# The mean square of a gated block: ones standing in four column groups, and a row turned back into a column

## The reference, cut to what matters

```
y = jnp.moveaxis(ys, 0, 1).reshape(b, l, D_INNER)          # D_INNER = 256
yn = y * jax.lax.rsqrt(jnp.mean(y * y, axis=-1, keepdims=True) + EPS) * norm_w
y = yn * jax.nn.silu(z)
return y @ Wout.T
```

## Time and profile before

| | |
|---|---|
| median of three runs | 737.92 us |
| the profiled execution's own time | 741.33 us |
| its span (first to last instruction) | 739.5 us |
| mean granted clock of TensorE | 0.967 |
| PE busy (TensorE, matmuls) | 661.4 us, 89% |
| PEld busy (TensorE, weight loads) | 542.4 us, 73% |
| DVE busy (VectorE) | 565.0 us, 76% |
| ACT busy (ScalarE) | 474.7 us, 64% |
| POOL busy (GpSimd) | 454.2 us, 61% |

### The profile page before, as it was taken

The page is one execution under the profiler, slowest core; times in us unless marked ns, Lnnn a source line. Parts: engine busy times, 40 slices in busy tenths (PEclk is TensorE's granted clock), DMA queues, the critical chain, the costliest instruction groups (busy, mean ns, idle before and its releaser), DMA issues.

```text
span 739.5 us, 19955 instructions
## 1 busy us (share of the span) xinstructions
PE 661.4 (89%) x5075; PEld 542.4 (73%) x5075; DVE 565.0 (76%) x1874; ACT 474.7 (64%) x1176; POOL 454.2 (61%) x648
## 2 busy tenths in 40 slices
PE   7978999999999999999998889999999999989800
PEld 5846766676666766676666579999999999988800
DVE  3388899989999999999999667667666667776644
ACT  3746767776687767676776437756655665666625
POOL 5023277777777777677776656767765555666643
PEclk9999999999999999999999799999999999999955
DMA  9180001110111011101110132333432224546243
GB/s 253 34 285 15 5 30 30 40 45 19 36 35 44 20 41 32 43 23 37 33 41 19 29 72 63 92 85 96 99 82 67 78 70 119 150 143 178 78 158 129
DMA packets 56399, 54.54 MB, mean 74 GB/s; under 512 B 9546, under 2 KB 45518, under 8 KB 56032
## 3 DMA queue, kind: packets, MB, share of 16 engines
q1 hardware_dynamic: 44704, 32.10, 16.4%
q0 software_dynamic: 8416, 16.93, 6.8%
q10 hardware_dynamic: 3168, 4.22, 1.6%
HBM read 31.05 MB, written 22.63 MB: 73 GB/s over the span
## 4 chain that ended last, share of the span: by engine, by line
PE 71%; DVE 11%; issue 9%; POOL 3%; DVEq 2%; ACT 2%; DMA 2%; SPq 0%; POOLq 0%; ACTq 0%
PE p L607 12%; PE pl L598 8%; PE pj L460 6%; PE p L598 4%; PE p L689 4%; PE p L659 4%; PE p L653 4%; PE p L697 3%; PE p L635 3%; PE pj L468 2%; PE p L668 2%; PE p L571 2%; PE p L557 2%; PE p L468 2%; PE pl L504 2%
## 5 line engine op out<-in xcount | busy, mean ns | idle before, releaser
L1634 POOL DMA_INDIRECT moe_rows<-xT x135 | 134.2, 994 | 91.2 <-DVE xT L1250 59.0
L1567 POOL DMA_INDIRECT sorted_rows<-pair,slot x128 | 128.7, 1006 | 32.5 <-issue 31.3
L1008 DVE SCALAR_TENSOR_TENSOR acc<-pj,conv_w_sb,acc 128x511 f32<-128x511 f32 (+2 forms) x192 | 142.4, 742 | 4.1 <-ACT acc L792 1.1
L607 PE MATMUL p<-w,xT 128*128 x1080 | 143.9, 276 | 1.8 <-DVE xT L1246 1.7
L927 ACT ACTIVATE xT<-pl,b_sb 128x128 f32<-128x128 f32 x360 | 103.1, 370 | 50.0 <-PE pl L598 48.4
L607 PEld LDWEIGHTS p<-w,xT 128*128 128x128 f32 x1080 | 132.0, 193 | 2.3 <-issue 2.2
L598 PE MATMUL pl<-xT 128*128 128x128 f32 x720 | 96.8, 278 | 2.4 <-DVE xT L1238 2.4
L598 PEld LDWEIGHTS pl<-xT 128*128 128x128 f32 x720 | 88.5, 194 | 3.1 <-issue 2.5
L1246 DVE TENSOR_TENSOR xT<-p,b_sb 128x128 f32<-128x128 f32 x135 | 39.1, 290 | 61.8 <-PE p L607 53.9
L792 ACT ACTIVATE acc<-pj,conv_b_sb,conv_w_sb 128x512 f32<-128x512 f32 x64 | 49.5, 773 | 33.5 <-PE pj L460 33.4
L927 ACT ACTIVATE xT<-p,b_sb 128x128 f32<-128x128 f32 x180 | 51.5, 370 | 25.1 <-PE p L598 24.1
(11 more groups left out here) (217 smaller groups left out, 1420.9 us busy)
## 6 DMA issues: line engine op xcount, KB each, us to landing
xT<-sorted_rows SPq DMA_DIRECT2D x135, 65.0 KB, 1.9
xres<-in_x SPq DMA_DIRECT2D x16, 256.0 KB, 3.1
w<-in_w SPq DMA_DIRECT2D x2, 2048.0 KB, 10.0
acc<-moe_rows SPq DMA_DIRECT2D x16, 256.0 KB, 4.0
xc<-moe_rows SPq DMA_DIRECT2D x16, 256.0 KB
out<-sz ACTq DMA_DIRECT2D x16, 256.0 KB, 2.4
moe_rows<-xT POOLq DMA_INDIRECT x135, 2.5
sorted_rows<-pair,slot POOLq DMA_INDIRECT x128, 2.6
```

The lines of the kernel that those rows point to most:

```text
L607: mm = pe.matmul(y_bank(j)[:, 0:P], hT[j % 4][:, f, :], w2[:, bass.ds(e, 1), f, :].rearrange("p e d -> p (e d)"), start=(f == 0), stop=(f ...
L1008: ins = dve.scalar_tensor_tensor(out=acc[:, k, j:TOKS], in0=pj[k % 2][:, 0:TOKS - j], scalar=conv_w[:, k, TAPS - 1 - j:TAPS - j], in1=acc[ ...
L1567: pool.indirect_dma_start(out=sorted_rows[:, :], out_offset=bass.IndirectOffsetOnAxis(slot[q.par][:, c, k:k + 1], 0), in_=(rowA, rowB)[k][ ...
L1634: pool.indirect_dma_start(out=moe_rows[:, :], out_offset=bass.IndirectOffsetOnAxis(xs[k][:, P:P + 1].bitcast(I32), 0), in_=ye[j % 8], in_o ...
```

## The change

The sums of squares now have 32 columns of ones standing and ysq moving, 128 columns of tokens. Chunk c writes to partitions 32c to 32c + 31, so each chunk has a column group of its own, and the loop over the two channel halves k is now the outer one. The result is a row of sums for each chunk, the same on 32 partitions. ScalarE copies the 128x128 block to `ssT` (`turn_sums`, right after the fourth square in ScalarE's order), TensorE turns it (a transpose, placed between the second and the third chunk of the w_out multiplications), and DVE reads one column of each 32 as ms, waiting for the turned block.

Beside it the semaphores x_in and yy_in are merged into one for each sequence, `seq_in`: the final additions wait for 16 + 32 = 48 on it in place of 32 on the old one.

```
+TURN_AT = 2
+        ssT = sb("ssT", [P, P])
-        x_in = [sem(f"x_in{i}") for i in range(SEQS)]
+        seq_in = [sem(f"seq_in{i}") for i in range(SEQS)]
...
-                    for c in range(NC):
-                        for k in range(CC):
-                            mm = pe.matmul(p7[:, c * PADN:(c + 1) * PADN], ysq[:, k, c * P:(c + 1) * P],
-                                           ones[:, 0:PADN], start=(k == 0), stop=(k == CC - 1))
+                    for k in range(CC):
+                        for c in range(NC):
+                            mm = pe.matmul(p7[Q * c:Q * (c + 1), 0:P], ones[:, 0:Q], ysq[:, k, c * P:(c + 1) * P],
+                                           start=(k == 0), stop=(k == CC - 1), skip_group_check=True)
                     mm.then_inc(ss_psum, 1)
                 if scan:
                     pe.wait_ge(g_ready, NC * (s.n + 1))
                     pe.wait_ge(Xdt_ready, NC * (s.n + 1))
                     for c in range(NC):
                         for k in range(CC):
+                            if (c, k) == (TURN_AT, 0):
+                                pe.wait_ge(ssT_ready, s.n + 1)
+                                pe.transpose(p7[:, P:2 * P], ssT[:, :], ident[:, :]).then_inc(turned_psum, 1)
...
+            def turn_sums(s):
+                act.wait_ge(ss_psum, s.n + 1)
+                wait(act, turned_psum, s.n)
+                act.copy(ssT[:, :], p7[:, 0:P]).then_inc(ssT_ready, 1)
...
                 if scan:
                     square(s, NC - 1)
+                    turn_sums(s)
...
                 if scan:
-                    dve.wait_ge(ss_psum, s.n + 1)
+                    dve.wait_ge(turned_psum, s.n + 1)
                     wait(dve, rms_ready, s.n)
-                    dve.tensor_scalar(ms[:, :], p7[:, 0:NC * PADN].rearrange("p (c e) -> p c e", e=PADN)[:, :, 0],
+                    dve.tensor_scalar(ms[:, :], p7[:, P:2 * P].rearrange("p (c e) -> p c e", e=Q)[:, :, 0],
                                       1.0 / DI, EPS, ALU.mult, ALU.add).then_inc(ms_ready, 1)
...
-                dve.wait_ge(yy_in[i], 32 * (n // FIN + 1))
+                dve.wait_ge(seq_in[n], 48)
...
-                pool.wait_ge(yy_in[i], 32 * (n // FIN + 1))
+                pool.wait_ge(seq_in[n], 48)
```

More of the change, by code:

```diff
@@ L286, in build @@
         scattered = [[sem(f"scattered_{'AB'[k]}{i}") for k in range(2)] for i in range(2)]
+        ssT_ready = sem("ssT_ready")
+        turned_psum = sem("turned_psum")
         table_step = sem("table_step")
@@ L299, in build @@
         (sT_psum, w1e_ready, h_psum, hT_ready, ye_psum, ye_ready) = [sem(n) for n in names_b]
-        yy_in = [sem(f"yy_in{i}") for i in range(FIN)]
         fin_out = [sem(f"fin_out{i}") for i in range(FIN)]
@@ L365, in _ @@
             for k in range(2):
-                dq.dma_start(land[k], x_seq[k]).then_inc(x_in[k], 16)
+                dq.dma_start(land[k], x_seq[k]).then_inc(seq_in[k], 16)
             for dst, name in ((w_xbc[:, :], "w_xbc"), (dt_bias[:, :], "dt_bias"), (conv_w[:, :, :], "conv_w")):
@@ L414, in load_moe @@
                 for k in range(2):
-                    dq.dma_start(yy[i][:, k], moe_seq[n, :, k]).then_inc(yy_in[i], 16)
+                    dq.dma_start(yy[i][:, k], moe_seq[n, :, k]).then_inc(seq_in[n], 16)
             dq.wait_ge(z_psum, CC * SEQS)
@@ L490, in enter_x @@
             def enter_x(q):
-                pe.wait_ge(x_in[q], 16)
+                pe.wait_ge(seq_in[q], 16)
                 wait(pe, xT_ready, q - 1)
```

## The result

756.89 us (755.58 to 757.74, 4 runs) against 738.81 (4 runs): ratio 1.0242, 95% interval 1.0219 to 1.0265, so 18.1 us slower where 15.3 more were forecast (753 on the 737.92 us of the first measurement; range 744 to 766). The profiled execution took 755.58 us, its span is 753.8; 14.3 more than the profiled execution of before.

A forecast was written before the change was run, and what follows sets the result against it. TensorE led the chain, but ScalarE, with 0.06 us to spare before the inner products, would bind. 12.6 (slots 1 to 13) + 1.3 (slot 0) + 0 (slot 14) + 1.4 (slot 15) = 15.3 us on 737.92 gave 753; range 744 to 766.

The forecast's parts named there:

- Four groups side by side, 0.66: Sums of squares on TensorE: 16 records in four column groups run as four steps, 0.66 us instead of 1.86 of loads.
- the other cases: Sums of squares on TensorE: 1.10 us if only two groups run together, 1.98 us if none do.
- The table load stays behind the copy: ScalarE: the table load before the Silus follows the copy, 1.03 us later: about 0.75 waiting, 0.29 copying.
- 0.97 a slot: Slots 1 to 13: inner products load 0.97 us later and each slot grows by that, 12.6 us in all.
- Slot 0, 1.3: Slot 0: decays' exponentials, between copy and Silus, start 1.47 us later, 0.2 of it slack: 1.3 us added.
- Slot 14, 0: Slot 14: ScalarE's 1.03 us delay disappears in existing waits of the fourth Silu and inner products: 0 us.
- ms, residual, merged semaphores at nothing: Slots 1 to 13: DVE reaches ms after the turned block is there, root and residual stay; merged semaphores cost 0 us.
- Slot 15, 1.4: Slot 15: the transpose stands behind w_out's wait for gt and half of w_out, so ms comes 1.4 us later.
- The load ahead of the square or the wait: Rivals on ScalarE: table load before the fourth square, 736.4 us, chance 0.08; before the wait for sums, 743.6, chance 0.05.
- fewer groups: Rivals for the sums: only two column groups at a time, 759 us, chance 0.21; none side by side, 772, chance 0.04.
- a clock that falls in every slot: Rival: TensorE's idle stretch ahead of the inner products halves its clock in every slot, 39 us more, 792; chance 0.06.
- The 0.06 of slack: ScalarE from fourth square to the inner products' weight load: only 0.06 us to spare, though 17.43 us busy of 24.

The follow-up runs named there:

- the second pair: Changed kernel and kernel before, both run and profiled again without edits: 756.83 us (ratio 1.0232) and 738.51 us (0.9999); profile spans 756.1 and 736.6.
- the second copy: Changed kernel with one more ScalarE copy of the same 128x128 block into a spare tile, ahead of the used one: 759.26 us, ratio 1.0262.
- slot 15 mended: Changed kernel with, in slot 15 only, the turn put ahead of w_out and its wait for gt: 753.28 us, ratio 1.0188.
- order of the Silus: Kernel before with the Silus in order 2, 3, 0, 1 and the inner products waiting for the first two alone: 738.76 us, ratio 0.9984.

## Why the prediction was right, and where it was short

- *Four groups side by side, 0.66.* Right: 0.64; and 1.07 and 1.94 for two and one agree with the steps of 0.11 that the other cases were built of (1.10 and 1.98).
- *The table load stays behind the copy.* Right. Measured from the square's end it moved by 1.03, as forecast: 0.76 of waiting and 0.28 of copying. Taking the copy off ScalarE (743), or only pulling the load ahead of the wait (746), takes most of the loss away.
- *0.97 a slot.* 0.97 at the inner products' load; 0.96 in the slot length. Slots 1 to 13 cost 12.4 us by the first pair of profiles and 12.6 by the second; 12.6 were forecast.
- *Slot 0, 1.3.* By the marks 0.98, and ms 0.24 later ahead of the first mark: 1.2.
- *Slot 14, 0.* Nearly: from its rms to the first load of the sums in slot 15 it takes 0.15 more in the second pair (0.23 in the first).
- *ms, residual, merged semaphores at nothing.* ms did not wait in slots 1 to 13, and with the copy on DVE, where the merged semaphores are still in, slots are back at 24.09.
- *Slot 15, 1.4.* The late turn was right, and the forecast of it too: at full clock ms comes 1.33 later behind the first load. What fell short is a term put at nothing, the clock, in slot 15 and behind it. In the second profile of the changed kernel w_out runs at half clock and ms comes 2.66 later, not 1.33. Then the experts: from rms to the first tile's matmuls the four profiles of the two kernels take 4.56 to 4.58, but the first Gelu comes 8.03 behind rms where the second profile of before has 7.10, because the first tile runs at half clock; the stretch (449.5 to 456.3) reaches past the first Gelu (453.7), and to the last one it takes 0.8 more. I had noted that PE's idle stretch in slot 14 grows, and put no price on what idle time does to the clock.
- *Why the clock falls there* stays open. In all seven profiles with the late turn (the changed kernel twice, the copy on DVE, the early table load, the second copy, one and two groups), TensorE is idle for 3.0 to 3.1 us ahead of the first tile, and the clock is at half for 3.4 or 6.8 us, from within 1.2 us of its first matmul. With slot 15 mended the idle time is 0.59 and it isn't, nor is it in the second profile of before (2.39). But in the first profile of before it is, for 3.4 us after 2.40. So the longer idle stretch goes with the longer stretch at half clock; none of these runs changed the clock alone, and length of idle time alone doesn't decide it.
- *The base.* The profiled execution of before, 741.33, lay above its timed runs, with 10.2 us at half clock between the roots of slots 14 and 15 (3.4 in its second profile), 3.4 more at the first tiles, and 1.2 more of waiting for the last rows. Part of slot 15's extra time was thus already in the rows that I measured against. In the second pair the account closes at 18.3 behind the first root (0.98 + 11.5 + 1.1 + 2.8 + 0.9 + 0.8 + 0.1). Of the 1.2 ahead of it, 0.24 is slot 0's, and about 0.7 goes with 3.4 us at half clock (46.7 to 50.1) that the second profile of the changed kernel has, ahead of the first sums of squares.
- *The rivals.* The load ahead of the square or the wait, fewer groups and a clock that falls in every slot did not occur: in both profiles the granted clock of slots 1 to 13 stayed at 1.00. Two readings behind the clock's case don't hold, though. It leaned on slot 0, where the clock stayed at 1.00 through an idle stretch; in five of the later profiles it fell at the end of that stretch, for 3.4 us (from 46.7 in the second profile of the changed kernel). And its price, 3 us more for 10 at half clock, stands in no row: the two profiles of before differ by 6.8 us at half clock and 1.3 us of time in slot 14 to 15. The 0.06 of slack that the forecast stood on is borne out: the table load moved by 1.03 and the inner products by 0.97. With ScalarE earlier (order of the Silus) the kernel before gains 0.16%, hardly more than a measurement can tell and nothing in its slots; and with the whole delay gone (the copy on DVE) the inner products still wait for ScalarE.

## What to carry to other kernels

Before moving a copy to an engine that is 64% busy, look at where in its order the copy will stand and what queues behind: here a wait of 0.76 us ahead of a function table load cost the slot all of it, while TensorE's saving of 0.9 had nowhere to go. A step may be placed where the queue has already done the urgent part: the same copy behind the table load and one Silu, with the two Silus that are waited for first, brought the slots from 25.07 to 23.89 us and, with slot 15's turn moved too, 1.024 to 0.995. Then look at the next queue; the last 0.3 us a slot lay on GpSimd, an engine that was idle a quarter of the slot. And profile a kernel twice before measuring against one profile: here two profiles of the same kernel differ by 2.9 us.

## What the runs showed of the hardware that I had not expected

- Four column groups in f32 with four different moving operands run at four times the rate of one: a record in each used group starts every 0.11 us, so 16 records take 1.94, 1.07 and 0.64 us in one, two and four groups, with 0.27 of each being the last record's own duration.
- In these rows ScalarE's instructions overlap their successors by about 0.1 us (copy to copy 0.16 apart at 0.27 each, copy to Silu 0.14), but not a table load (copy to load 0.28). So the copy costs 0.28 ahead of a table load and 0.14 behind it.
- The same kernel gives different stretches at half clock from one execution to the next: 10.2 and 3.4 us between the roots of slots 14 and 15 in two profiles of the kernel before, worth 1.3 us, and one of 3.4 us at the first tiles in one of them alone.
